# Basis matrices loaded in 2 KB pieces of 16 neighbouring rows, relation weights read back 16 rows at a time, and two adjacency loads moved ahead of the weights

## The reference

```python
def rgcn_gate_layer(x, row, col, edge_type, basis, att, gate_w, root, bias):
    w = jnp.einsum('rb,bio->rio', att, basis)        # basis: 30 x 512 x 512
    x_j = x[col]
    msgs = []
    for r in range(NUM_RELATIONS):
        gate = jax.nn.sigmoid(x_j @ gate_w[r, :, 0])
        msgs.append(gate[:, None] * x_j @ w[r])
    msg = jnp.where((edge_type == 0)[:, None], msgs[0], msgs[1])
    agg = jax.ops.segment_sum(msg, row, num_segments=x.shape[0])
    return agg + x @ root + bias
...
h = jax.nn.relu(rgcn_gate_layer(x, row, col, edge_type, basis1, att1, gate_w1, root1, bias1))
out = rgcn_gate_layer(h, row, col, edge_type, basis2, att2, gate_w2, root2, bias2)
```

## Time and profile before

| | |
|---|---|
| median of 3 runs | 2353.74 us |
| lowest and highest run | 2352.77 and 2354.81 us |
| the profiled execution | 2352.55 us |
| its span, first to last instruction | 2350.8 us |
| around the span | 1.75 us |
| PE busy in the span | 2202.4 us (94%) |
| mean granted TensorE clock | 0.98 |

### The profile page before, as it was taken

One profiled execution on the slowest core, in us unless ns is written; L12 is line 12 of the kernel. 1 busy time (PEld: TensorE's weight loads), 2 busy tenths in 40 slices (PEclk: granted clock), 3 DMA queues, 4 the chain that ended last, 5 costly groups with the idle time before them and its releaser, 6 DMA issues.

```text
span 2350.8 us, 36257 instructions
## 1 busy us (share of the span) xinstructions
PE 2202.4 (94%) x13797; PEld 1899.8 (81%) x13797; DVE 1593.8 (68%) x3322; ACT 1119.3 (48%) x1806; POOL 546.2 (23%) x401
## 2 busy tenths in 40 slices
PE   2889968999999999999999999999999999999998
PEld 1456647899988889988888998898899888877887
DVE  9989986478776458877646887763787774244233
ACT  5146652377743347763335775233677533222321
POOL 6000000066510026650003663000566200000000
PEclk9899978999999999999999999999999999999999
DMA  9899963111031011003102003111110421062034
GB/s 253 220 250 253 274 203 123 44 31 44 1 113 66 21 52 44 22 37 101 52 20 65 22 23 98 64 37 31 44 44 1 134 73 29 17 103 43 1 69 105
DMA packets 110945, 189.56 MB, mean 81 GB/s; under 512 B 57893, under 2 KB 58341, under 8 KB 103099
## 3 DMA queue, kind: packets, MB, share of 16 engines
q1 hardware_dynamic: 106776, 180.47, 28.9%
q10 hardware_dynamic: 4003, 6.79, 1.1%
HBM read 155.16 MB, written 32.07 MB: 80 GB/s over the span
## 4 chain that ended last, share of the span: by engine, by line
PE 75%; DVE 11%; issue 5%; ACT 5%; DMA 2%; DVEq 1%; SPq 1%; POOL 0%; ACTq 0%; POOLq 0%
PE PS L1043 10%; PE PS L1071 9%; PE PS L962 6%; PE PS L964 6%; PE PS L963 6%; PE PS L1057 6%; PE PS L948 5%; PE PS L952 4%; PE PS L949 4%; PE PS L1199 4%; PE PS L1209 4%; PE PS L859 3%; PE PS L812 2%; ACT prob L1433 1%; DMA basis_t<-in_L_gnn_basis_dram 1%
## 5 line engine op out<-in xcount | busy, mean ns | idle before, releaser
L793 POOL TENSOR_SCALAR prob<-prob,inv_den 125x1000 f32<-125x1000 f32 x160 | 444.5, 2778 | 0.0
L781 POOL TENSOR_TENSOR rstd<-var_eps,neg_half 125x2 f32<-125x2 f32 x45 | 35.4, 787 | 907.1 <-DVE var_eps L1596 907.1
L1433 ACT ACTIVATE prob<-prob,neg_max 125x1254 f32<-125x1254 f32 x160 | 215.5, 1347 | 56.9 <-DVE neg_max L1936 56.7
L1931 DVE CUSTOM_DVE_ANT_0 prob<-PS,sbias 125x1254 f32<-125x1254 f32 x160 | 233.0, 1456 | 11.0 <-issue 8.4
L1071 PE MATMUL PS<-pT_hi,v_hi 125*128 125x250 f32 x800 | 236.0, 295 | 0.0
L1950 DVE TENSOR_TENSOR pT_lo<-PS,pT_hi 125x1000 fp32r<-125x1000 f32 x160 | 191.1, 1194 | 51.2 <-ACT pT_hi L1450 51.2
L1071 PE MATMUL PS<-pT_lo,v_hi 125*128 125x250 f32 x800 | 224.1, 280 | 0.0
L1071 PE MATMUL PS<-pT_hi,v_lo 125*128 125x250 f32 x800 | 222.3, 278 | 0.0
L1057 PE MATMUL PS<-ident,prob 125*125 125x125 f32 x1600 | 201.7, 273 | 5.6 <-DVE pT_lo L1953 5.5
L1057 PEld LDWEIGHTS PS<-ident,prob 125*125 125x125 f32 x1600 | 196.1, 189 | 12.6 <-issue 7.6
L1448 ACT ACTIVATE pT_hi<-PS 125x1000 fp32r<-125x1000 f32 x160 | 161.8, 1011 | 82.7 <-PE PS L1057 82.7
(11 more groups left out here) (330 smaller groups left out, 5628.2 us busy)
## 6 DMA issues: line engine op xcount, KB each, us to landing
basis_t<-in_L_gnn_basis_dram SPq DMA_DIRECT2D x80, 768.0 KB, 12.5
sbias<-score_bias SPq DMA_DIRECT2D x40, 548.6 KB
adj<-adj SPq DMA_DIRECT2D x20, 546.9 KB
w_lo_raw<-in_L_gnn_m_w_dram SPq DMA_DIRECT2D x8, 1024.0 KB, 6.5
score_bias<-biases SPq DMA_DIRECT2D x10, 548.6 KB
adj<-count SPq DMA_DIRECT2D x10, 546.9 KB
xc<-x_lat SPq DMA_DIRECT2D x12, 448.0 KB
x_first<-x_lat SPq DMA_DIRECT2D x10, 448.0 KB
```

What stands on the lines that cost most here:

```text
L793: pool.tensor_scalar(prob[u % 3][:, 0:SPLIT], prob[u % 3][:, 0:SPLIT], inv_den[0:T, u % 4:u % 4 + 1], None, ALU.mult)\
L1433: act.activation(prob[u % 3][:], prob[u % 3][:], ACT.Exp, bias=neg_max[0:T, u % 4:u % 4 + 1], accum_out=den[0:T, u % 4:u % 4 + 1]).then_in ...
L1931: v.tensor_tensor_reduce(prob[u % 3][:].rearrange("p (j s) -> p j s", j=3), PS[0:T, 0:3, 0:SB], sbias[p % 2][a][:].rearrange("p (j s) -> p ...
```

## The change

Three edits, all on SP but for two counts of semaphores.

1. A basis load is four transfers instead of one. Block j of partition 6i+b now holds row 16j+i of the stretch, so each transfer takes, of each of six matrices, 16 neighbouring rows as 2 KB pieces; before, one piece was four neighbouring rows, 8 KB. The bytes and the destination tile are the same, and PE waits for four times the count.
2. `load_r` reads 16 rows in one transfer, four times as many transfers: 32 for a relation instead of 8. The row order in `rel_w` changes with edit 1, and the 16 rows are neighbours on both sides.
3. After the first relational layer's products, `load_adj(2)`, `load_adj(3)` and `load_adj(4)` each stand ahead of one `load_r(1, n)`, instead of behind all three.

```diff
@@ load_r
                     for k in range(D // GR):
-                        p0 = GR * (k % 2)
-                        sp.dma_start(wr_raw[n][p0:p0 + GR, k // 2, :],
-                                     rel_w[l, k, :, :].rearrange("(j r i) d -> r i j d", j=4, r=R)[n]).then_inc(rel_in[n], 16)
+                        for j in range(4):
+                            p0 = GR * (k % 2) + GROUP_I * j
+                            at = GROUP_I * (R * j + n)
+                            sp.dma_start(wr_raw[n][p0:p0 + GROUP_I, k // 2, :], rel_w[l, k, at:at + GROUP_I, :]).then_inc(rel_in[n], 16)
@@ load_bases
-                sp.dma_start(basis_t[n % RING][:], rows.rearrange("b (i j) d -> i b (j d)", j=4)).then_inc(basis_in[n % RING], 16)
+                for j in range(4):
+                    sp.dma_start(basis_t[n % RING][:, j, :], rows[:, GROUP_I * j:GROUP_I * (j + 1), :].rearrange("b i d -> i b d"))\
+                        .then_inc(basis_in[n % RING], 16)
@@ the end of SP's program
                 sp.wait_ge(r_mm_ps, 3 * NT * (l + 1))
-                if l == 0:
-                    for n in range(3):
-                        load_r(1, n)
                 for t in range(NT):
                     n = NT * l + t
                     if n + 2 < 2 * NT:
                         sp.wait_ge(r_adj_lo, n + 1)
                         load_adj(n + 2)
+                    if n < 3:
+                        load_r(1, n)
@@ relation_loads on PE
-                    pe.wait_ge(basis_in[load % RING], 16 * (load // RING + 1))
+                    pe.wait_ge(basis_in[load % RING], 64 * (load // RING + 1))
@@ r_high on ACT
-                act.wait_ge(rel_in[n], 16 * (l + 1) * (D // GR if n < R else 1))
+                act.wait_ge(rel_in[n], 16 * (l + 1) * (4 * D // GR if n < R else 1))
```

## The result

The changed kernel takes 2359.98 us (median of 7 runs, 2359.41 to 2362.91), the kernel before, on the same chip, 2352.43 (2348.58 to 2354.81). The ratio is 1.0038, with a 95% interval of 1.0026 to 1.0050: about 8 us slower, where 4 us faster was forecast. The time lies inside the range that was given, 2339 to 2363 us, but by luck: the range was drawn for rivals A, B and part of C, and none of these is what happened. The two profiled executions are 10.4 us apart (spans of 2361.2 and 2350.8 us).

A forecast was written before the change was run, and what follows sets the result against it. PE, busy 94% of the span, was taken to bound the kernel, so transfers matter only where PE stands still. Slower loads (+0.9) and reordered counts (-4.6) summed to -3.7 us: 2350.0 us, 8-in-10 range 2339 to 2363 us.

The forecast's parts named there:

- A: Whole kernel: loads stay near 247 GB/s, counts ahead of the weights give net 4.6 us less; 2350.0 us, chance 0.43.
- B: Setup: basis loads go towards 353 GB/s and the sorting part gives 9.1 us; 2340 us, chance 0.32.
- C: Setup: 2 KB pieces are slower, 215 GB/s or 3.90 us per load, 20 us more; 2369 us, chance 0.12.
- Edit 2 takes part of it back: First relational layer's aggregation: 32 issues at 0.35 us take 11.2 us, tile 4 stalls 1.6 us; costs 2.5 us.
- D: Aggregation: 16-row issues cost SP 0.63 us, tiles 3 and 4 stall 6.4 and 13.1 us; 2370.5 us, chance 0.07.
- rival Q: Aggregation, posed with the experiments: the weights' transfers themselves, however issued, hold up the adjacency loads; no chance given.
- Edit 3: Aggregation, before tile 2: counts ahead of the weights remove the stall and slow first group, 7.1 us less.
- x_c[2]: Last attention layer: its load moves to about 1863.6 us behind 32 transfers; counted zero, up to 2 us to lose.
- Edit 1: Setup: basis loads in 2 KB pieces run at 247 GB/s, 3.39 us per load; 0.9 us more.
- The sum: Whole kernel: 0.9 - 4.6 = -3.7 us, giving 2350.0 us against the median.

The follow-up runs named there:

- e2_order_alone: The kernel before with only the order of issue changed, counts ahead of the weights; 2345.79 us, ratio 0.9972.
- e6: The kernel before with each basis load in four transfers of 2 KB pieces, rows still 8 KB apart; 2349.43 us, ratio 0.9986.
- e4: The kernel before with only the basis loads in 2 KB pieces of neighbouring rows, read-back in 8 transfers of 64 rows, old issue order; 2366.94 us, ratio 1.0059.
- h: The kernel before with each basis load in six transfers of 16 rows, 8 KB pieces kept; 2387.65 us, ratio 1.0138.
- s1_spread: The kernel before with only the cut basis loads, each weight read back in 8 transfers with 16 rows outermost; 2353.33 us, ratio 1.0003.
- e1: The changed kernel with only the read-back put back to 8 transfers of 64 rows per weight, in the new row order; 2353.09 us, ratio 0.9997.

## Why the prediction was wrong, step by step

**The step that failed is the price of a 16-row issue**, in "Edit 2 takes part of it back": 310 ns from line 502, "the row nearest to their form". Line 502 has two rows of that very form in the trace of the kernel before, and the prediction looked at the lower one. The other, in the same answer:

```profile
L502 SPq DMA_DIRECT2D raw_b<-in_L_gnn_s_w_dram x8: 327/421/983, 320.2 to 1556.6; - x8
```

The eight issues of this row took 327, 327, 327, 340, 502, 967, 977 and 983 ns. So the form had no one price, and "eight rows at 310 ns in the very form" was no argument against D, since the eight others stood beside them. That their median of 421 ns is what the changed kernel paid is chance: it lies halfway between 340 and 502, and none of them took it. The 310 ns rows each follow an issue of one row (line 503). In the four chains of 32 like issues SP took 411 to 430 ns for 121 of the 128; the other seven are 342 and 343 (each the first of a chain), 489 to 523, and 1490 and 1571. With the 0.04 us gap 420 is 0.46 us, above the threshold of 0.41 which rival D itself gave. No trace from before the change has a chain of this form, so the price was open between 310 and 983 ns; the step took the lowest value there was.

**D was the right mechanism, at a price between the two.** At 0.467 us the stalls are 3.40 and 6.48 us, not D's 6.4 and 13.1. The price alone does not make the first of them: 32 issues took 3.75 us longer than the 11.2 of the sum, which had 2.6 us in hand before tile 3, and that leaves 1.15. The rest are two terms that were a little small: the pair of counts ahead of the weights cost SP 3.22 us, not 2.25, and PE started tile 3 10.22 us after its counts' first issue, not 9.14. That last 1.08 us is the most that rival Q can have at this tile. D had a chance of 0.07, which rested on those eight rows alone.

**Edit 3: right.** Tile 2's stall and slow group went; e2_order_alone gave 2345.79 us where the step's arithmetic, 7.1 us off, leads to about 2347.

**`x_c[2]`: wrong by the same price.** The prediction moved its load to 1863.6 us, "zero, with up to 2 us to lose". With 0.50 us per issue, the one of 1490 ns included, it started 15.9 us after the first weight, at 1865.64, in a kernel whose uses were 2.6 us earlier by then. DVE waited 2.77 us and the lower clock behind it made 5.5 of that. A wait of DVE cost PE twice its length here, and the sum had no term for this.

**Edit 1: wrong in rate, wrong in what it is worth.** The rate was 288 and 302 GB/s, not 247. The rows that should be alike (partitions under 128) were not what bound the loads, so rival B's mechanism, faster loads, is what happened, though for another reason: e6 shows that neighbouring rows are not needed. B's 9.1 us did not come in full: the brackets gave 8.0, and 3.6 of them went again, since the prediction took DVE to be at work in all the rest. In the kernel before, its rows of 3.73, 11.00 and 4.17 us hold 12.3 us of standing still that no bracket shows, in the changed kernel such rows hold 15.8. In the profiles, three kernels (the changed one, e4 and h) had the long form of 14.4 us and the others that keep the memset had that of the kernel before, e2 a little shifted. SP's time for each of the four transfers of a basis load was 0.597 us in the median, 0.56 expected. B also called SP's issuing enough where its own numbers have 6.7 us of it in a batch of 6.4.

**The sum** read with what the two profiled executions show: -2.6 us in the setup (forecast +0.9), +5.5 at `x_c[2]` (0), -7.1 at tile 2 (-7.1), +14.6 at tiles 3 and 4 (+2.5): 10.4 us.

## What to carry to other kernels

Price a run of transfers by its issues on the queue that also carries something urgent: count them, take the duration that such issues have in a run of their own kind, and compare with the slack of what stands behind. Where the trace has no such run, look at every issue of that form and not at one row's median: here they spread from 310 to 983 ns, and the rival that starts at 410 was worth more than 0.07. Before cutting or reordering a transfer, look at the outermost dimension of both sides; with four steps in it on one side, four DMA engines did the work of 16 here. And an instruction that takes several times its usual duration may be standing still, though the profile calls it busy: look at what another engine finishes at the same moment.

## What the runs showed of the hardware that I had not expected

- A read-back of 64 rows with the outermost dimension of 4 instead of 16 has 5 completion events, not 16, and landed up to 14.65 us after its issue; e4, which has it, took 13.6 us longer than s1_spread. With such transfers under way SP stood 8.77 and 9.70 us in the two issues of a count in e1, in place of 2.25.
- Transfers into 16 partitions of four 2 KB pieces each keep the DMA engines full at 139 to 145 GB/s, where cut basis loads into 96 partitions reach 279 to 304 from 100 to 135 us.
- From 100 to 135 us the same basis loads run at 296 GB/s in two transfers, at 279 to 304 in four, and at 254 and 262 in one (the kernel before and e2_order_alone). Whether the 8 KB piece or the single transfer is the cause is open.
- VectorE stood still for up to 13.2 us behind GpSimd's memset and the product before it. In these profiles it comes in two forms, 10.5 and 13.2 us together: in one a tensor_tensor is caught, which comes free between the two GpSimd instructions (45.29, 3.73 us), in the other a tensor_scalar (43.83, 14.62 us), which has to wait for both. What decides between them is open; the recorded start of GpSimd's product does not (42.76 and 43.15 us in kernels of the short form, 42.96 and 43.33 in kernels of the long one).
- SP's issue time does not follow bytes or rows: 16 rows of 2 KB 420 ns, 16 rows of four such pieces 426, 64 rows 594 in one order and 510 in the other, 16 rows of 8 KB 589, and 310 ns for 16 rows of 2 KB right behind a one-row transfer. These are medians; in the same form single issues took up to 1.5 us.
